# Cross-attention block on one core: softmax denominators through a DRAM scratch in 128-byte runs, and another order of the DMAs on SyncE

## What is computed

```python
def _attention(xq, xkv, wq, wk, wv, wo, bo):
    q = (xq @ wq).reshape(B, S, N_HEADS, D_HEAD)
    k = (xkv @ wk).reshape(B, T, N_HEADS, D_HEAD)
    v = (xkv @ wv).reshape(B, T, N_HEADS, D_HEAD)
    attn = jnp.einsum('bihd,bjhd->bhij', q, k) * scale
    attn = jax.nn.softmax(attn, axis=-1)
    out = jnp.einsum('bhij,bjhd->bihd', attn, v).reshape(B, S, D_ATTN)
    return out @ wo + bo

h = _layernorm(x, ln1_g, ln1_b)
x = _attention(h, h, sa_wq, sa_wk, sa_wv, sa_wo, sa_bo) + x
h = _layernorm(x, ln2_g, ln2_b)
x = _attention(h, cond_emb, ca_wq, ca_wk, ca_wv, ca_wo, ca_bo) + x
h = _layernorm(x, ln3_g, ln3_b)
p = h @ ff_w1 + ff_b1
a, gate = (p[..., :D_FF], p[..., D_FF:])
h = a * jax.nn.gelu(gate, approximate=False) @ ff_w2 + ff_b2
return h + x
```

## Time and profile before

| | |
|---|---|
| median of 3 runs | 3643.42 us (3624.12 to 3646.33) |
| profiled execution | 3645.71 us |
| its span | 3643.9 us |
| busy: PE, DVE, ACT, POOL | 62%, 37%, 32%, 28% of the span |
| mean granted clock of TensorE | 0.781 of 2.4 GHz |
| DMA packets | 326999, 237.57 MB |

### The profile page before, as it was taken

How to read it: one execution, slowest core, us unless ns; L and a number is a source line. 1 busy time by engine, 2 the same in 40 slices (tenths; PEclk the granted TensorE clock), 3 DMA queues, 4 the chain that set the end, 5 groups by cost and what they waited for, 6 DMA issues and landing times.

```text
span 3643.9 us, 41988 instructions
## 1 busy us (share of the span) xinstructions
PE 2265.4 (62%) x13824; PEld 2179.0 (60%) x13824; DVE 1359.1 (37%) x2394; ACT 1159.9 (32%) x3256; POOL 1002.5 (28%) x1727
## 2 busy tenths in 40 slices
PE   5655665665655566556566555566566665555999
PEld 5655655565655566555555555566565555555888
DVE  3332333333333333333333333333333333333665
ACT  3332333333333333333333333333333333332211
POOL 3333233322222222223233333222222222222110
PEclk8777777777777777777777777777777777777999
DMA  5433434433333333334443444433333243332000
GB/s 121 69 69 73 70 70 70 73 73 67 67 61 61 61 61 64 61 68 71 63 72 71 73 76 72 73 70 70 70 64 64 64 66 64 67 64 40 24 30 18
DMA packets 326999, 237.57 MB, mean 65 GB/s; under 512 B 169728, under 2 KB 291968, under 8 KB 326784
## 3 DMA queue, kind: packets, MB, share of 16 engines
q1 hardware_dynamic: 326784, 234.89, 34.8%
HBM read 58.08 MB, written 8.91 MB: 18 GB/s over the span
## 4 chain that ended last, share of the span: by engine, by line
DMA 58%; SPq 24%; PE 14%; issue 3%; DVE 1%; ACT 0%; POOL 0%; DVEq 0%; POOLq 0%; ACTq 0%
DMA denominators<-RDEN 54%; SPq L912 8%; SPq L910 8%; SPq L929 7%; DMA RING<-RING 4%; PE PTB L712 2%; PE S L712 2%; PE QKB L297 2%; PE PTB L270 2%; PE VB L725 1%; PE QKB L725 1%; PE S L258 1%; PE S L259 1%; PE WOP L311 1%; PE VB L331 1%
## 5 line engine op out<-in xcount | busy, mean ns | idle before, releaser
L258 PE MATMUL S<-RING 128*128 128x256 f32 x1024 | 445.8, 439 | 1338.1 <-DMA RING<-RING 1338.1
L258 PEld LDWEIGHTS S<-RING 128*128 128x128 f32 x1024 | 311.9, 305 | 1389.3 <-DMA RING<-RING 1389.3
L469 DVE TENSOR_REDUCE NM<-S 128x4 f32<-128x1024 f32 x256 | 313.5, 1225 | 1776.7 <-PE S L259 1776.7
L390 ACT ACTIVATE PH<-PTB 128x1024 fp32r<-128x1024 f32 x256 | 262.6, 1026 | 2044.1 <-PE PTB L270 2044.0
L623 POOL TENSOR_TENSOR ON<-ON,RB 128x256 f32<-128x256 f32 x256 | 186.1, 727 | 2042.6 <-DMA RB<-denominators 1986.5
L403 ACT ACTIVATE PT<-S,NM 128x256 f32<-128x256 f32 x1024 | 478.6, 482 | 10.9 <-DVE NM L469 10.9
L270 PE MATMUL PTB<-IDN,PT 128*128 128x128 f32 x2048 | 456.0, 399 | 0.0
L259 PE MATMUL S<-RING 128*128 128x256 f32 x1024 | 406.8, 401 | 0.0
L270 PEld LDWEIGHTS PTB<-IDN,PT 128*128 128x128 f32 x2048 | 402.2, 214 | 0.0
L502 DVE TENSOR_TENSOR PL<-PTB,PH 128x1024 fp32r<-128x1024 f32 x256 | 313.4, 1224 | 120.1 <-ACT PH L390 116.4
L259 PEld LDWEIGHTS S<-RING 128*128 128x128 f32 x1024 | 322.8, 315 | 0.0
(11 more groups left out here) (104 smaller groups left out, 3247.6 us busy)
## 6 DMA issues: line engine op xcount, KB each, us to landing
RING<-RING SPq DMA_DIRECT2D x512, 192.0 KB, 3.5
RING<-RING SPq DMA_DIRECT2D x512, 128.0 KB, 3.6
RB<-denominators SPq DMA_DIRECT2D x512, 64.0 KB, 3.6
out_dram<-XR SPq DMA_DIRECT2D x32, 256.0 KB, 6.9
XR<-in_x_dram SPq DMA_DIRECT2D x16, 256.0 KB, 7.3
denominators<-RDEN SPq DMA_DIRECT2D x256, 2.0 KB, 8.8
XR<-out_dram SPq DMA_DIRECT2D x16, 256.0 KB, 5.6
CX<-in_ctx_dram SPq DMA_DIRECT2D x16, 192.0 KB, 7.8
```

Of the source, the lines that this page charges most:

```text
L258: e.matmul(o, q, RX[:, c % 2, i, K1, :], start=True, stop=False)
L390: e.activation(PH[:, :], PTB[:, :, :].rearrange("p i n -> p (i n)"), ACT.Copy) \
L469: e.tensor_reduce(NM[:, :].rearrange("p (i t) -> p i t", t=TT), S1[:, :, :].rearrange("p i (t s) -> p i t s", t=TT), AX.X, ALU.max, negate ...
```

## The change

The tile `RDEN` becomes 128 x 32, set to 1.0 at the start, and the reciprocals go to its first 4 columns. A new VectorE instruction transposes it in blocks of 32 x 32 into `RDT` (two buffers): partition 32 b + j of `RDT` then holds, for j < 4, the reciprocals of column j for the 32 positions of block b. The store sends all 128 partitions, each as one run of 128 bytes, into a scratch of 32 x 128 per buffer, of which the first four rows are read back. `save_den` waits for the transpose (`dve_rt`), and the transpose for the reciprocals. In SP's loop, `save_den(c-1)` and `spread_den(c-1)` come first and `copy_ring(c+2)` after them, before the large transfers.

```diff
-        RDEN = sb("RDEN", [P, 2, 4])
+        RDEN = sb("RDEN", [P, 32])
+        RDT = sb("RDT", [P, 2, 32])
...
-        DS = nc.dram_tensor("denominators", (4, 2, TT, P), F32, kind="Internal").ap()
+        DS = nc.dram_tensor("denominators", (4, 32, P), F32, kind="Internal").ap()
...
-                e.reciprocal(RDEN[:, s % 2, :], DEN[:, s % 2, :]).then_inc(a.dve_rc, 1)
+                e.reciprocal(RDEN[:, 0:4], DEN[:, s % 2, :]).then_inc(a.dve_rc, 1)
+                sl.wait(e, a.dve_rc, s + 1)
+                e.transpose(RDT[:, s % 2, :], RDEN[:, :]).then_inc(a.dve_rt, 1)
...
             def save_den(s):
 
-                e.wait_ge(a.dve_rc, s + 1)
+                e.wait_ge(a.dve_rt, s + 1)
                 if s >= 4:
                     e.wait_ge(d_rb[s % 2], 32 * ((s - 4) // 2 + 1))
-                e.dma_start(DS[s % 4, :, :, :].rearrange("i t p -> p (i t)"), RDEN[:, s % 2, :],
-                            allow_slow_non_contiguous=True).then_inc(d_ds[s % 4], 16)
+                e.dma_start(DS[s % 4, :, :].rearrange("j (b r) -> b j r", b=4),
+                            RDT[:, s % 2, :]).then_inc(d_ds[s % 4], 16)
...
                 for i in range(2):
                     e.dma_start(RB[OWN[i], s % 2, :],
-                                DS[s % 4, i, :, :].rearrange("t p -> (t p)").partition_broadcast(P // 2)) \
+                                DS[s % 4, TT * i:TT * (i + 1), :].rearrange("t p -> (t p)").partition_broadcast(P // 2)) \
                         .then_inc(d_rb[s % 2], 16)
...
-            for c in range(-1, ATT + 2):
-                if 0 <= c - 2:
-                    spread_den(c - 2)
-                if c + 1 < ATT:
-                    copy_ring(c + 1)
-                if 0 <= c - 1 < ATT:
+            for c in range(-2, ATT + 1):
+                if c >= 1:
                     save_den(c - 1)
+                    spread_den(c - 1)
+                if c + 2 < ATT:
+                    copy_ring(c + 2)
                 weights(c)
                 spill(c)
...
+            e.memset(RDEN[:, :], 1.0).then_inc(s_ring, 1)
```

More of the change, by code:

```diff
@@ L178, in __init__ @@
                 self.dve_rc = sem("dve_rc")
+                self.dve_rt = sem("dve_rt")
                 self.dve_pl = sem("dve_pl")
```

## The result

The changed kernel takes 2057.22 us, median of 3 runs (2053.68 to 2062.23), against 3643.42 us: a ratio of 0.566, 95% interval 0.562 to 0.569. The forecast was 2380 us with a range of 2140 to 2800.

The account below looks back on a forecast made before the run. SP's loop of save, landing, spread and copies was taken to bound the kernel. Landing 3.5, issuing 4.17 and large transfers 0.35 gave 8.02 us a pair; 256 pairs plus 325 us outside gave 2380 us, range 2140 to 2800.

Parts of the forecast that it names:

- The bound: SP's loop of save, landing, spread and copies sets the time, 12.97 us a pair before; no compute engine is at its limit.
- The large transfers: Weights, spill and similar loads and stores on SP's queue, now ahead of the save, add 0.35 us a pair to the landing.
- Packets of the save: The store's landing falls from 8.8 to 3.5 us: some 3 us behind four copies, then a short receipt.
- rival 3: Shorter landing of 2.6 us, 6.8 to 7.1 us a pair, 2110 us; chance 0.11 for under 2220 us.
- the longer dependence: From save through copy and scores to the save two pairs later: 14.5 us, 7.25 us a pair, below the SP loop.
- Order on SP: SP's new issue order alone gains nothing; copies go a pair earlier, and large transfers lose the cover of the landing.
- VectorE: 256 transposes of 0.2 us each, 51 us in all, lie in VectorE's idle time and delay nothing.
- PE: Matmuls take near 6 us in most pairs as waits shrink and the clock rises above 0.9, so PE doesn't bind.
- rival 1: PE takes over if its clock falls back at every short wait: 8.9 us a pair, 2603 us; chance 0.14.
- Rivals 2, 4 and 5: Store's tail: partly stays, 2890 to 3400 us (0.16); four engines keep it, 3735 us (0.04); no effect, 3646 us (0.03).

Follow-up runs that it names:

- e10: The changed kernel with the large transfers (weights, spill) issued between the store and the read instead of ahead of the store: 1988.49 us, ratio 0.504.
- e11: The changed kernel itself, unaltered, run again in the third later session: 2067.81 us.
- e3: The changed kernel with an outer dimension of 128 instead of 4 in the store's pattern: 2073.56 us.
- e1: The changed kernel with SP's loop put back to the order of before, so the new store alone: 1989.38 us, ratio 0.505.
- e2: The kernel before with SP's new order alone, keeping the store of 4-byte runs: 4004.14 us, ratio 1.017.
- e7: As e1, but from the fifth pair on each of the 128 runs has 32 bytes instead of 128: 1986.72 us.
- e6: The kernel before with its 512 runs of 4 bytes each in 128 bytes of its own in the scratch: 2077.43 us, ratio 0.527.
- e5: The kernel before, storing from the fifth pair on only 32 of 128 partitions, 128 runs of 4 bytes instead of 512: 2828.64 us, ratio 0.718.
- e4: The changed kernel with the ring copies issued between the store and the read of the scratch: 1888.43 us, ratio 0.479.
- e12: As e6, but with a distance of 32 bytes between the 4-byte runs instead of 128: 2112.08 us.
- e13: As e6, but with a distance of 64 bytes between the 4-byte runs instead of 128: 2086.87 us.

## Why the prediction was right or wrong

*The bound.* Right. The loop of save, landing, spread and copies bounds both kernels; only its length changed, and all outside the pairs stayed at 325 us.

*The sum, term by term.* Predicted 3.5 + 4.17 + 0.35 = 8.02 us a pair, measured 6.75. The large transfers, 0.35, measure 0.31 (e10 against e11). The landing without them, 3.5, is 2.34 in the pair shown (1002.08 to 1004.42), and 2.3 is the median in e3, where the profile gives it. What is left for issuing is 6.75 - 2.34 - 0.31 = 4.10, predicted as 4.17. So of the 325 us too many, (3.5 - 2.34) x 256 = 297 come from the landing.

*The step that failed* is "Packets of the save": 3.5 us of landing, "still behind four copies (some 3 us), and then a short receipt". The landing was 2.3 us, and the step had two faults. The first is the size of the queue: the 3 us in which packets pass in the earlier trace rows are not what the copies add to a landing. Four copies add 0.9 us, to the 1.4 us of a store with nothing ahead (e3). The trace of the kernel before could have told: its last two stores have no copies ahead, and take as long as any. The first of them is issued at 3336.34, and the view from 3336.3 to 3346 has:

```profile
denominators<-RDEN SPq DMA_DIRECT2D x1, 2.0 KB, 9.0
```

From the second, at 3348.84, to its read are 8.0 us. The second fault is the price: the neighbours whose 3.5 to 3.6 us I took as the nearest had been lengthened by the very stores that the change removes. With these gone they land in 2.9 and 2.6 us. The lower bound of the same step, 2.4 us from the large store with nothing ahead, came out as the measured value, but by chance: it stood for a store of 256 KB alone, and the new one has 16 KB and four copies ahead.

*The range.* Its lower end came from rival 3, which stopped at the longer dependence, (2.6 + 11.0) / 2 = 6.8 us. That too was summed from rows of the kernel before: first copy to first matmul is now 1005.64 to 1010.55, 4.9 us instead of 6.0, and from the first matmul to the end of the transpose it is 2.8 us (1004.16 to 1006.97) instead of 3.8. I had used a piece of the earlier trace rows from a pair with a granted clock of 0.77 in a chain that was to hold for pairs at 1.00. In rows of the changed kernel the dependence is 2.34 + 1.22 + 4.91 + 2.81 = 11.3 us, or 5.6 us a pair (an estimate from one pair). So no floor stood where I put one; SP waited for the transpose only 4.7 us in all.

*Order on SP.* Right: the cycle is the same, a copy issued a pair earlier gives nothing, and the large transfers lose their cover (e1, e2, e10). The forecast did not draw the conclusion that the old order would have been better with the new store.

*VectorE.* Right: 256 transposes of 0.21 us, and SP waited for them 4.7 us in all.

*PE and rival 1.* Right that it stays at 2.4 GHz when its waits are short. Two stretches of the changed kernel (the third number from the end is the granted clock) and the matmuls with which three pairs begin, the wait in brackets:

```profile
1004.00:1010.40 6.40, 5.67 (x46) 5.47 (x46) 4.91 (x10) 3.85 (x12) 2.92 (x6) 1.00 0.58 145
...
1024.00:1032.00 8.00, 5.93 (x37) 5.93 (x38) 4.45 (x8) 3.51 (x10) 6.59 (x12) 0.79 0.58 147
```

```profile
1004.16 0.39 PE L260 MATMUL S<-RING 128*128 128x256 f32 x1 [1.17 <-DMA RING<-RING]
...
1010.55 0.39 PE L260 MATMUL S<-RING 128*128 128x256 f32 x1 [0.71 <-DMA RING<-RING]
...
1026.07 0.39 PE L260 MATMUL S<-RING 128*128 128x256 f32 x1 [2.45 <-DMA RING<-RING]
```

The clock is 1.00 behind the waits of 1.17 and 0.71 us (the second pair, 1010.50 to 1016.80, has 1.00 too), and these pairs have 5.7 to 5.9 us of matmuls, as the pair without a wait in the earlier trace rows. In the stretch around the wait of 2.45 us it is 0.79, and the 7.5 us from 1026.0 on have 7.4 us of matmuls at 0.77. The ring copies of that pair came after a landing of 3.4 us with large transfers ahead. So what rival 1 describes does occur, but seldom enough that the mean clock is 0.983 and SP's loop sets the time.

*Rivals 2, 4 and 5* rested on a tail priced per store or per engine. The size of the runs, their count and the outer dimension were all varied, and none of these alone makes the tail: not the size (e7), not 512 packets (e6), not the outer dimension (e3). 512 runs of 4 bytes side by side do, and the same runs 32 bytes apart don't. The Trainium skill ("DMA: Bandwidth & Descriptors", section "Specifications") says that below 512 B a DMA engine does a read-modify-write; the prediction worked out from it a tail of 1.5 us for 128 short runs. The runs show no such tail: e7 (128 runs of 32 bytes) lands in 2.3 us, and e6 with 512 short runs in 2.7 us. That neighbours wait for one another on the same few bytes is what fits all of these runs. With the distance the whole stretch of DRAM grew too, from 2 KB to 16 KB and more, and the two were not varied apart. In e5 fewer runs lie side by side within nearly the same stretch, and the tail is shorter, so the stretch alone does not make it. How DRAM or the DMA engine does this, no trace shows.

## What to carry to other kernels

When a DMA's landing is long, look for a stretch without packets ahead of its semaphore; if there is one, look at where the bytes go before you look at how many they are. Price a changed transfer not by neighbours that suffered from the old one. Before you blame part of a landing on what stands ahead in the queue, look in the trace for the same transfer with nothing ahead; the first or last rounds of a loop often have one. And when a serial loop through a queue bounds the kernel, put work of the same queue, here the ring copies, under the landing: that gave another 9% (e4 against e11).

## What the runs showed of the hardware that was not expected

- 512 stores of 4 bytes land in 9.9 us when they lie side by side in 2 KB of DRAM, in 2.8 us when 32 bytes apart, 2.7 us at 64 or 128 (e2, e12, e13, e6).
- Such stores slow other DMAs of the queue: the SBUF-to-SBUF copies of 192 KB land in 3.5 us (kernel before), 4.0 us (e2) and 4.1 us (e5, a quarter of the runs), in 2.9 us without such stores, and in 3.0 us beside 512 runs that are 128 bytes apart (e6).
- A store of 16 KB in 128 runs, alone in the queue, lands in 1.4 us; four copies of 640 KB directly ahead make it 2.3 us (e3).
- The first measurement and four later sessions, on four chips, differ by 8% on the kernel before (3643 against 3932 to 3948 us; landing 8.8 us, and 9.9 us in e2), and by 0.5% on the changed one (2057.22 and 2067.81 us).
- TensorE's granted clock was 1.00 in pairs behind waits of 0.71 and 1.17 us, where the stretch around a wait of 2.45 us had 0.79 and the pair behind one of 5.73 us 0.77: with the waits, PE also lost 452 us of busy time.
